# Attention's set-up block dissolved into the attention program: loads first, ones written by DMA, four PSUM banks for the first unit

## What is computed

```python
def _mha(x, ctx, mask, qw, qb, kw, kb, vw, vb):
    q = _split_heads(x @ qw + qb)
    k = _split_heads(ctx @ kw + kb)
    v = _split_heads(ctx @ vw + vb)
    scores = jnp.einsum('bqhd,bkhd->bhqk', q, k) / np.sqrt(D // H)
    if mask is not None:
        scores = scores + mask
    out = jnp.einsum('bhqk,bkhd->bqhd', jax.nn.softmax(scores, axis=-1), v)
    return out.reshape(x.shape[0], x.shape[1], D)

ca = _mha(layernorm(x), ctx, mask, cq_w, cq_b, ck_w, ck_b, cv_w, cv_b)
x = self_output(ca, layernorm(x), co_w, co_b, co_g, co_be)
sa = _mha(x, x, None, sq_w, sq_b, sk_w, sk_b, sv_w, sv_b)
x = self_output(sa, x, so_w, so_b, so_g, so_be)
```

## Time and profile before

| | us |
|---|---|
| median of three runs | 1977.41 |
| the three runs | 1977.00, 1977.41, 1981.69 |
| span of the profiled execution, from its first to its last instruction | 1978.4 |
| TensorE busy in the span | 1788.8 |
| VectorE (DVE), ScalarE (ACT), GpSimd (POOL) busy | 1404.5, 1221.4, 1217.9 |

### The profile page before, as it was taken

The page is one execution under the profiler, slowest core; times in us unless marked ns, Lnnn a source line. Parts: engine busy times, 40 slices in busy tenths (PEclk is TensorE's granted clock), DMA queues, the critical chain, the costliest instruction groups (busy, mean ns, idle before and its releaser), DMA issues. The chain is left out here.

```text
span 1978.4 us, 36354 instructions
## 1 busy us (share of the span) xinstructions
PE 1788.8 (90%) x12326; PEld 1325.6 (67%) x12326; DVE 1404.5 (71%) x2786; ACT 1221.4 (62%) x2305; POOL 1217.9 (62%) x1117
## 2 busy tenths in 40 slices
PE   0799999999999999999985999923999999999995
PEld 0455555555555555555545888923999999999995
DVE  5378788787887878888833877844667667766762
ACT  0167777676776767777753554413777777777773
POOL 6635657565665744556336466551787778878775
PEclk9999999999999999999987999956999999999998
DMA  3665554665655565555412122126667667666762
GB/s 93 120 136 118 123 133 106 118 139 123 135 114 125 106 128 130 124 126 108 83 60 73 49 102 76 70 80 219 216 212 231 215 210 226 220 222 208 230 216 33
DMA packets 125198, 274.80 MB, mean 139 GB/s; under 512 B 15803, under 2 KB 57915, under 8 KB 124629
## 3 DMA queue, kind: packets, MB, share of 16 engines
q1 hardware_dynamic: 110708, 253.77, 47.0%
q0 software_dynamic: 14304, 18.72, 4.7%
HBM read 196.50 MB, written 75.92 MB: 138 GB/s over the span
## 5 line engine op out<-in xcount | busy, mean ns | idle before, releaser
L706 DVE TENSOR_REDUCE nz<-ps 128x1 f32<-128x512 f32 x1024 | 650.8, 684 | 182.9 <-PE ps L845 180.9
L620 ACT ACTIVATE spare<-ps 128x512 f32<-128x512 f32 x1024 | 571.3, 601 | 267.1 <-PE ps L855 263.0
L1743 POOL TENSOR_TENSOR u_lo<-u_f,u_hi 128x256 fp32r<-128x256 f32 x273 | 376.8, 1397 | 142.4 <-ACT u_hi L1777 142.3
L1849 PE MATMUL ps_e<-x_hi,we_hi 128*128 128x256 f32 x1092 | 312.9, 287 | 4.9 <-DVE we_lo L1663 4.9
L1849 PE MATMUL ps_e<-x_lo,we_hi 128*128 128x256 f32 x1092 | 305.7, 280 | 0.0
L1849 PE MATMUL ps_e<-x_hi,we_lo 128*128 128x256 f32 x1092 | 305.7, 280 | 0.0
L855 PEld LDWEIGHTS ps<-qst,kst 52*128 52x128 f32 x1024 | 102.0, 184 | 277.3 <-ACT spare L620 189.8
L867 PE MATMUL ps<-spare,vaug 128*32 128x512 f32 x2048 | 274.9, 609 | 0.0
L845 PE MATMUL ps<-kst,qst 50*128 50x512 f32 x1024 | 264.1, 442 | 10.9 <-issue 10.1
L855 PE MATMUL ps<-qst,kst 52*128 52x512 f32 x1024 | 269.2, 501 | 3.7 <-ACT spare L620 3.3
L1703 DVE TENSOR_TENSOR u_f<-ps_e,silu 128x256 f32<-128x256 f32 x273 | 115.1, 422 | 180.9 <-ACT silu L1808 176.3
(11 more groups left out here) (224 smaller groups left out, 3620.0 us busy)
## 6 DMA issues: line engine op xcount, KB each, us to landing
we_raw<-in_experts_w SPq DMA_DIRECT2D x117, 896.0 KB, 4.9
parts_kept<-parts SPq DMA_DIRECT2D x64, 512.0 KB, 3.9
kst<-parts_kept SPq DMA_DIRECT2D x192, 128.0 KB, 4.3
qst<-parts_kept SPq DMA_DIRECT2D x192, 128.0 KB, 5.3
x_raw<-xs SPq DMA_DIRECT2D x39, 259.0 KB, 2.8
maxima<-nsplit SPq DMA_DIRECT2D x64, 128.0 KB, 3.5
x<-sum_tok SPq DMA_DIRECT2D x16, 512.0 KB, 2.7
x_tok<-x SPq DMA_DIRECT2D x16, 512.0 KB, 4.1
```

Of the source, the lines that this page charges most:

```text
L620: act.activation(probs[:, e % 8], ps[:, score_bank(e, par)], ACT.Exp, scale=SCALE).then_inc(exp_made, 1)
L706: dve.tensor_reduce(nz[:, g % 2, place:place + 1], ps[:, max_bank(m, par)], AX.X, ALU.max, negate=True).then_inc(max_made, 1)
L1743: pool.tensor_tensor(u_lo[:, it], u_f[:, q % UPS], u_hi[:, it].bitcast(F32), ALU.subtract).then_inc(ulo_made, 1)
L1849: ins = pe.matmul(ps[:, q % UPS, c * GR:(c + 1) * GR], left, right, start=m == 0, stop=m == len(terms) - 1)
```

## The change

The set-up block goes. Its temporaries become parts of tiles that are not in use yet (`w_raw` lies in `spare`, `mask_raw` in `ev`, `mask_hi` and `mask_lo` in `sum_tok`, `v_bias` in `at_tok`, `folded` in a PSUM bank of `ps`), and its work goes into each engine's `start`. ACT issues the weight loads in three pieces, the columns and the rows, and makes the high halves of ctx and of the weights. The ones are written by four transfers from a small row of ones. The first unit's normalisation moves from POOL to DVE. The first unit's items take four PSUM banks in turn. SP's order becomes: store K, load K, store Q, load Q. `item` on ACT and TensorE now takes the bank itself instead of its distance from `MISC`; those lines are left out.

```diff
+WEIGHT_LOADS = ((0, 2), (2, 4), (4, 8))
+WEIGHT_ORDER = (1, 0, 2, 3, 4, 5, 6, 7)
...
 def start_banks():
-    return in_turn([START_ITEMS], MISC_BANKS)[0]
+    return in_turn([START_ITEMS], 4)[0]
...
-    with nc.sbuf_tensor("w_raw", [P, 8, KD, D], F32) as w_raw, \
...
-            nc.semaphore("mask_kept") as mask_kept, nc.Block() as block:
...
+    START_BANKS = (MISC, SCORE, SCORE + 1, SCORE + 2)
...
@@ block.sync @@
             def start(now, after):
                 load_x(0, *now)
                 load_ctx(0)
+                sp.wait_ge(mask_zero, 1)
+                sp.dma_start(mask_raw[0:B, :], A["mask"]).then_inc(mask_raw_in, 16)
+                load_x(1, *after)
+                sp.wait_ge(ones_made, 1)
+                ones = ones_row[:, :].unsqueeze(1).to_broadcast([2, 2 * NP_, S])
+                for stack, first in ((kst, MAX_ROW), (qst, MASK_ROW)):
+                    for half in range(2):
+                        row = BLOCK * half + first
+                        sp.dma_start(stack[row:row + 2].rearrange("r k a n -> r (k a) n")
+                                     .bitcast(F32), ones).then_inc(ones_in, 16)
+                sp.wait_ge(mask_hi_made, 1)
+                sp.dma_start(scratch["masks"][0], mask_hi.bitcast(F32)).then_inc(mask_kept, 16)
+                sp.wait_ge(mask_lo_made, 1)
+                sp.dma_start(scratch["masks"][1], mask_lo.bitcast(F32)).then_inc(mask_kept, 16)
+                sp.wait_ge(mask_kept, 32)
                 load_mask(0, 0, *now)
-                load_x(1, *after)
                 for mt in range(2):
                     for kq in range(2):
                         keep_parts(0, kq, mt)
-                    for kq in range(2):
                         load_stack(0, 0, kq, mt)
...
@@ block.gpsimd @@
             def start(now, after):
                 places = {name: stage for name, _, stage in start_banks()}
-                for name in ("ctx0", "norm", "ctx1", "in0", "in1", "k0", "q0", "k1", "q1", ">norm",
-                             "resid", "max0", ">in0", ">in1", ">ctx0", ">ctx1", ">resid", "max1"):
+                pool.wait_ge(ctx_in, 16)
+                first_ctx(0)
+                pool.wait_ge(half_made, 1)
+                root(0, x_var, x_root, 1)
+                first_ctx(1)
+                root(0, x_var, x_root, 2)
+                low_of_weights((2,))
+                for name in ("in0", "in1", "k0", "q0", "k1", "q1"):
+                    item(name, places[name], 0, *now)
+                low_of_weights(range(3, 8))
+                pool.wait_ge(rows_folded, 2)
+                for name in ("resid", "max0", ">in0", ">in1", ">ctx0", ">ctx1", ">resid", "max1"):
...
@@ block.scalar @@
             def start(now, after):
+                load_weights(0)
+                act.dma_start(cols[:, :], A["cols"]).then_inc(cols_in, 16)
+                load_weights(1)
+                load_weights(2)
+                for n in ATTN_ROWS:
+                    act.dma_start(rows[n][:, :], A[n].partition_broadcast(P)).then_inc(rows_in, 16)
+                first_ctx(0)
+                high_of_weights((0,))
+                first_ctx(1)
+                high_of_weights((1, 2))
+                act.wait_ge(cols_in, 16)
...
+                    if name == "v0":
+                        high_of_weights(range(3, 8))
+                        act.wait_ge(cleared, 2)
...
@@ block.vector @@
             def start(now, after):
-                for b in range(2):
-                    for step in range(QT + 1):
-                        x_moments(step, b, b)
+                dve.memset(mask_raw, 0.0).then_inc(mask_zero, 1)
+                dve.memset(ones_row[:, :], 1.0).then_inc(ones_made, 1)
+                dve.memset(neg_half[:, :], -0.5).then_inc(half_made, 1)
+                dve.memset(nz[:, :, :], 0.0)
+                for step in range(QT + 1):
+                    x_moments(step, 0, 0)
+                split_mask()
+                low_of_weights((0,))
+                first_norm(0, 0)
+                low_of_weights((1,))
+                for step in range(QT + 1):
+                    x_moments(step, 1, 1)
...
+                dve.memset(vaug[:, :, :, :, :], 0.0).then_inc(cleared, 1)
+                dve.wait_ge(cleared, 1)
+                dve.memset(vaug[:, :, :, :, DH:DH + 1], 1.0).then_inc(cleared, 1)
+                first_norm(1, 1)
+                fold_rows()
                 for m in range(LEAD):
                     reduce_max(0, m, 0)
...
@@ block.tensor @@
             def start(now, after):
+                taken.update({bank: [] for bank in START_BANKS})
                 for name, place, _ in start_banks():
+                    if name == "k0":
+                        pe.wait_ge(w_lo_dve, 1)
+                    if name == "q0":
+                        pe.wait_ge(w_lo_dve, 2)
+                    if name == "v0":
+                        fold_bias()
+                        pe.wait_ge(w_lo_pool, 1)
...
+                    if name == "v1":
+                        pe.wait_ge(ones_in, 64)
                     for m in START_MAXIMA.get(name, ()):
                         maximum(0, m, 0)
+                pe.wait_ge(w_lo_pool, 6)
...
```

More of the change, by code:

```diff
@@ L147, in attention_phase @@
     nzt = sb("nzt", [P, 2, QT * 32])
-    with nc.sbuf_tensor("w_raw", [P, 8, KD, D], F32) as w_raw, \
[L150 to L160, removed]
-            nc.semaphore("mask_kept") as mask_kept, nc.Block() as block:
[L162 to L216, removed]
-        @block.gpsimd
-        def _(pool):
-            pool.memset(kst[32:64, :, :, :].bitcast(F32), 1.0).then_inc(ones_made, 1)
-            pool.wait_ge(ones_made, 1)
-            pool.memset(kst[96:128, :, :, :].bitcast(F32), 1.0).then_inc(ones_made, 1)
-            pool.wait_ge(ones_made, 2)
-            for j in range(1, 8, 2):
-                pool.wait_ge(hi_made, j + 1)
-                pool.tensor_tensor(w_lo[:, j], w_raw[:, j], w_hi[:, j].bitcast(F32), ALU.subtract)
@@ L603, in end @@
                 held.update({n: [] for n in range(STAGES)})
-                for name, bank, stage in end_banks():
-                    item(name, bank, stage, u, *now, u % 2)
+                for name, place, stage in end_banks():
+                    item(name, MISC + place, stage, u, *now, u % 2)
             def period(u, par, now, before, after, after2):
@@ L622, in period @@
                         if half == 0:
-                            for name, bank, stage in late:
-                                item(name.strip("<>"), bank, stage,
+                            for name, place, stage in late:
+                                item(name.strip("<>"), MISC + place, stage,
                                      *whose(name, u, now, before, after, after2),
@@ L718, in turn_max, with first_norm @@
                     .then_inc(nz_turned, 1)
-            def start(now, after):
-                for b in range(2):
-                    for step in range(QT + 1):
-                        x_moments(step, b, b)
+            def first_norm(u, b):
+                dve.wait_ge(x_root, b + 1)
+                for qt in range(QT):
+                    x = x_tok[:, u % KEPT, qt]
+                    dve.tensor_scalar(x, x, mv[:, 0, qt, 0:1], rstd[:, 0, qt:qt + 1],
+                                      ALU.subtract, ALU.mult).then_inc(x_normed, 1)
@@ L755, in _ @@
         def _(pe):
-            taken = {n: [] for n in range(MISC_BANKS)}
+            taken = {}
             def frees(name, u, b):
@@ L890, in period @@
                     last.append((in_up, 2 * KD))
-                taken.update({n: list(last) for n in range(MISC_BANKS)})
+                taken.update({MISC + n: list(last) for n in range(MISC_BANKS)})
                 banks = period_banks(before, after, after2)
@@ L904, in period @@
                     for name, place, _ in banks[s]:
-                        item(name.strip("<>"), place, *whose(name, u, now, before, after, after2))
+                        item(name.strip("<>"), MISC + place,
+                             *whose(name, u, now, before, after, after2))
                     if s % 2:
```

100 lines of the change are left out of this document (89 added, 11 removed).

## The result

The changed kernel takes 1947.51 us (median; 1944.45 to 1949.84, four runs) against 1977.2 (1975.54 to 1981.69, four runs): 29.7 us less, a ratio of 0.9842 with an interval of 0.9817 to 0.9866. The forecast was 1954.0 in a range of 1944 to 1963. Its profiled execution took 1946.28 us with a span of 1944.3.

The account below looks back on a forecast made before the run. TensorE fills the attention stage, so only the 100.5 us ahead of the first score counts, in three chains: -34.7 + 2.2 + 9.1 = -23.4 us, from a 1978.4 us span to 1955.0, as median 1954.0; range 1944 to 1963.

Parts of the forecast that it names:

- rival A: SP's alternating stores and loads cost nothing, first k store to first score stays 41.6 us: 1945 us; chance 0.17.
- chain (c): First k store to first score, 41.6 us before: alternating SP's stores and loads adds 9.1 us, bounds 0, +12.
- Chain (a): Set-up block ahead of x's load: removed, so what stood at 36.49 us starts at 1.82, -34.7 us.
- Chain (b): From x's load to the first k store, 22.5 us before: 24.7 after, +2.2 us, bounds -1 and +4.5.
- The new wait: POOL's second root stands ahead of in0, so the first unit's splits wait for the second unit's statistics, to 17.0 us.
- The stall: POOL's splits held by DVE instructions through the shared port pair before the first k store: 1.5 us, between nothing and 3.5.
- The ones and the masks: SP's transfers ahead of the first k store: ones done at 17.3, masks by 20.5, 6 us of cover, cost 0.
- The upper bound: Ones on two engines at 8.4 each take 15.5 us, to 27.3; masks end at 30.3, holding the store 3.8 us.
- B: SP held by the ones on two slow engines, 3.8 to 8 us late: 1958 to 1962 us; chance 0.15.
- C: Set-up work stays on the path and pushes the first k store to 36 us: 1963.5 us; chance 0.04.
- D: Ones use a single engine, 31 us, masks by 46, 19.5 late: 1973.5 us, no change; chance 0.03.
- E: Ones at half one engine's rate take 61 us and hold SP's stores: slower, 2004 us; chance 0.03.

Follow-up runs that it names:

- the second profile: The changed kernel run once more without any edit, in the same call as three others: 1949.86 us, ratio 0.9842 to the kernel before.

## Why the prediction was right, and where it was not

**What bounds the kernel**: right, as the table above shows to within some us: what counts is the first score.

**The number**: the time lies in the range because the range took in most of rival A; the sum itself was 6.5 us too high, by chain (c). That is luck of the range and not of the working. (A run's time is 1.6 to 2.1 us above its span in the runs that give both, so the 1.0 us that the sum takes from span to median mixes two things; the forecast is the median before less 23.4 either way.)

**Chain (a), -34.7**: right to 0.1 us. What was moved out of it found its cover: bias fold and v are done by 35.7 and POOL's five subtracts by 46.8, ahead of the first maxima's split.

**Chain (b), +2.2**: measured +2.9, as the first store goes at 27.14 (forecast 26.5). Its parts hold. The new wait, POOL's second root ahead of in0, stands there with 3.89 us of idle time, and the edit that moves it, with the low half behind it, brings k0's halves 3.4 us forward. Four banks buy nothing, as costed. The stall was put at 1.5 us: POOL's first root takes 1.50 for 1.04, its first subtract 1.46 for 1.26 (1.27 in the second profile), and DVE's normalisation 2.42 for 1.6, which is 1.5 together on the path. The sum without a stall came to 25.0 and the store stands at 27.14, so another 0.6 us lies in small differences. Also, DVE's low half beside POOL took 1.61 us and the next one, with POOL idle, 0.68. The Trainium skill, page "SBUF — State Buffer", section "Who interferes with whom", states that a VectorE instruction with two inputs in SBUF contends with a GpSimd instruction that reads SBUF; these two durations agree with it.

**Chain (c), +9.1**: the step that failed. Measured +0.7 (42.3 us from the first store to the first score, 41.6 before). The term at fault is "a store is back 4.1 us after issue on an empty queue (58.95 to 63.06)". The row behind it, in the earlier trace rows, is a group of two stores; the second waited for POOL's halves of q, and SP's waits of the kernel before, from 56 to 66 us, say so: 21.5 us in two waits, of which one is the 18.2 ahead of the first store, which leaves 3.3 for the second.

```profile
SPq L353 <- POOL parts L463: 21.5, 2, 18.2
```

A store is back after 2.79 us in the changed kernel (2.78 in four others). That is 1.3 us less at each of the four returns of parts in the chain, and the round trips come out shorter than costed, counted from the first store T: q known at T + 11.6 (forecast 14.4), k1 at + 21.9 (26.0), q1 at + 30.5 (36.2). The maxima's store was known at + 38.3 (46). So 5.2 of the 8.4 us too much come from this one misread row, added up along the chain. The maxima's store makes 2.3 (4.75 us in place of 7), and the four loads behind it 0.7 (4.0 in place of 4.7). With SP's old order put back the same stretch takes 41.1 us, so what the alternation costs is 1.2.

**The ones and the masks, cost 0**: right in its sum, wrong in its working. The text took 5.5 us for 256 KB, by a tail in the earlier trace rows, and 6 us of cover; the runs show 8.1 us per 256 KB, the maskings' load issued by 25.19 in place of 20.5, and 1.9 us of cover. The tail was misread: if it is the end of the two-row mask loads, as the text took it, these had been issued some 5 us before it began (the line below is from SP's timeline of the kernel before), so it shows what was left of them and not how long they took.

```profile
37.38 0.60 SPq L346 DMA_DIRECT2D kst<-masks  x2
```

The upper bound (two engines at 8.4 GB/s each, ones to 27.3, masks to 30.3) was as far off on the other side: by the DMA view the ones ended between 22 and 24. The Trainium skill's page "DMA: Bandwidth & Descriptors", section "Why a DMA increments its semaphore by 16 and not by 1", has the rule of two engines for two rows; the DMA views of both widths agree with it.

**The rivals.** A (the alternation costs nothing, 1945) was nearer than the forecast: with nothing for chain (c) and the measured +2.9 for (b) it gives a span of 1946.6 us (1978.4 - 34.7 + 2.9), against the 1944.3 of the profiled execution; the 31.1 us by which the first score moved are within 0.7 of it. It deserved more than 0.17: what was held against it, two more returns of a store, was priced by the misread row. B, C, D and E did not happen. B's mechanism did: SP waits 12.4 us behind the ones. It cost nothing because they were done earlier than B's bound (maskings by 25.19, not 30.3) and because POOL's second root held k0's halves to 27.10; with the root moved away the ones do hold the store, by 1.4 us.

## What to carry to other kernels

A group of two transfers in a timeline is not one transfer's duration: before a gap is used as a price, ask the view of waits what the issuing engine waited for in it. Work taken off the front of a program is worth its full time only up to the next thing that is late; here POOL's second root and, once that is moved, a transfer of ones into two rows, behind which 18 KB wait 12 us. Judge an edit at the start by the time stamp at which the steady stage begins, which differed by 0.07 us between two profiles of one kernel, and not by the total, whose runs spread over 10 us. And see in each kernel whether what lies ahead of the edit has moved.

## What had not been expected of the hardware

- A small transfer (18 KB) behind one of two rows took over 12 us to be known, and issuing slowed with it: 1.29 us for two transfers of ones into q's stack, but 4.98 for the last two of eight, with the ones doubled.
- TensorE's granted clock was 0.50 (1.2 of 2.4 GHz) in the whole stretch of the first maxima, 46.89 to 69.45, behind 11.19 us of idling; before it was 1.00 there, behind 3.56 us. No cost shows: the stretch took 22.56 us for 22.40, and the 34 products took 799 ns each in both. DVE's reductions, 16 in 9.66 us, are busy for most of the stretch (20.36 us) and likely set the pace.
